# Conditioning in column groups, scans of two segments with ScalarE carries, unpadded heads in layer 3

## Time and profile before

| | |
|---|---|
| three runs | 8062.61, 8064.74 (median), 8066.53 us |
| profiled execution | 8064.97 us; its span, first to last instruction, 8063.2 us |
| busy in the span | PE 7071.7 us (88%), PEld 3761.9, DVE 6189.8 (77%), ACT 5870.7 (73%), POOL 2286.7 (28%) |
| mean granted clock of TensorE | 0.954 of 2.4 GHz |

### The profile page before, as it was taken

The page is one execution under the profiler, slowest core; times in us unless marked ns, Lnnn a source line. Parts: engine busy times, 40 slices in busy tenths (PEclk is TensorE's granted clock), DMA queues, the critical chain, the costliest instruction groups (busy, mean ns, idle before and its releaser), DMA issues. The chain is left out here.

```text
span 8063.2 us, 233691 instructions
## 1 busy us (share of the span) xinstructions
PE 7071.7 (88%) x94272; PEld 3761.9 (47%) x94272; DVE 6189.8 (77%) x4829; ACT 5870.7 (73%) x7834; POOL 2286.7 (28%) x1375
## 2 busy tenths in 40 slices
PE   7999588888888888888888888887989999979998
PEld 5444244444444444444444444444435454535554
DVE  2555499999999999999999999998434353445554
ACT  2555499999999999999999999996224343435544
POOL 0000133333333333333333333332003232323332
PEclk9999699999999999999999999998999999989999
DMA  4666522222222222222222222222520000000000
GB/s 151 151 155 146 117 70 67 64 68 67 70 66 66 67 68 69 66 66 68 67 67 66 68 68 67 67 64 98 200 81 9 6 9 8 6 32 9 12 11 6
DMA packets 621116, 541.43 MB, mean 67 GB/s; under 512 B 490224, under 2 KB 528752, under 8 KB 606448
## 3 DMA queue, kind: packets, MB, share of 16 engines
q1 hardware_dynamic: 620032, 526.35, 22.5%
HBM read 380.72 MB, written 145.49 MB: 65 GB/s over the span
## 5 line engine op out<-in xcount | busy, mean ns | idle before, releaser
L1267 DVE TENSOR_TENSOR_SCAN s_h<-s_decay,s_h 128x1040 f32<-128x1040 f32 x2048 | 4623.9, 2336 | 33.8 <-ACT s_decay L1191 33.8
L1162 ACT COPY s_h<-s_pb 128x1024 f32<-128x1024 f32 x2048 | 2506.0, 1224 | 111.1 <-PE s_pb L1093 92.2
L1106 PE MATMUL s_py<-s_h,s_cz 128*32 128x128 f32 x32768 | 2512.9, 436 | 6.1 <-DVE s_h L1267 6.1
L1191 ACT ACTIVATE s_decay<-s_pa 128x1024 f32<-128x1024 f32 x2048 | 2139.4, 1045 | 123.6 <-DVE s_h L1267 53.4
L1234 POOL TENSOR_TENSOR s_h<-s_h,s_one 128x64 f32<-128x64 f32 x384 | 875.3, 2279 | 2079.3 <-DVE s_h L1267 2079.3
L1078 PE MATMUL s_pa<-s_dl,s_al 18*128 18x64 bf16 x32768 | 857.8, 192 | 673.7 <-ACT s_decay L1191 584.9
L1106 PEld LDWEIGHTS s_py<-s_h,s_cz 128*32 128x32 f32 x32768 | 1036.5, 123 | 469.3 <-issue 10.0
L1078 PEld LDWEIGHTS s_pa<-s_dl,s_al 18*128 18x128 bf16 x32768 | 612.8, 95 | 1019.9 <-ACT s_decay L1191 953.4
L1093 PEld LDWEIGHTS s_pb<-s_ul,s_bl 18*128 18x128 bf16 x16384 | 475.3, 95 | 1031.3 <-ACT s_h L1162 877.5
L1093 PE MATMUL s_pb<-s_ul,s_bl 18*128 18x128 bf16 x16384 | 838.1, 222 | 27.7 <-ACT s_h L1162 16.0
L1222 POOL TENSOR_TENSOR s_cz<-s_cl,s_one 128x128 f32<-128x128 f32 x256 | 434.3, 1697 | 964.2 <-PE s_py L1106 952.4
(11 more groups left out here) (223 smaller groups left out, 6219.2 us busy)
## 6 DMA issues: line engine op xcount, KB each, us to landing
s_bl<-B SPq DMA_DIRECT2D x1024, 72.0 KB
s_ul<-U SPq DMA_DIRECT2D x1024, 72.0 KB
s_dl<-D SPq DMA_DIRECT2D x1024, 72.0 KB
s_al<-A SPq DMA_DIRECT2D x256, 144.0 KB
D<-p_dp SPq DMA_DIRECT2D x64, 384.0 KB, 6.5
U<-p_up SPq DMA_DIRECT2D x64, 384.0 KB, 5.6
B<-p_bz SPq DMA_DIRECT2D x144, 128.0 KB, 2.2
SZ<-p_sz SPq DMA_DIRECT2D x16, 1024.0 KB, 5.1
```

The source lines that it names most:

```text
L1106: mm = pe.matmul(py[e % 2][QR * q:QR * q + QR, 0:P], cz[e % 2][:, l * P + QR * q:l * P + QR * q + QR], states, start=(l == 0), stop=(l == ...
L1162: act.copy(out, pb[:].rearrange("p b t d -> p d b t")).then_inc(bu_done, 1)
L1191: act.activation(decay[(STEPS * e + 2 * z + j) % RING][:, :, 1:W], pa[j % 2][:], ACT.Exp).then_inc(exp_done, 1)
L1267: dve.tensor_tensor_scan(seg, decay[(STEPS * e + 2 * z + j) % RING][:].rearrange("p d w -> p (d w)"), seg, 0.0, ALU.mult, ALU.add).then_in ...
```

## The change

**conditioning.** `cond`, `hid` and `sil` are padded to 32 columns and become the weights everywhere: the 4096 outputs of `w2a` and `w2b` are cut into four groups of 1024, `mod` into three of 1536, and each group writes its own 32 partitions of PSUM. `w2a` and `mod` are then turned back by transposes. SP loads `w2a` and `w2b` ahead of `wm`, PE does `mod` last. `az` outlives the stage, and its 18 stores stand in `prepare` behind `reload(0)`. POOL sets the zeros and the identity.

**scan.** A scan covers STRIDE = 2 steps, 2080 elements, HALVES = 4 scans a tile; `decay` has RING = 3 buffers of 32 channels x 65, the same memory. The carry is ACT's, in two copies of 64 channels after the exps of steps 0 and 4, for the tiles that have one before them in their sequence. POOL zeroes column 0 of the first tile of a sequence in one operation, and keeps the fill.

**transformer.** Layer 3 has HR = 16: HT = 8 heads a tile, MT = 2, PT = 4. The padded arrays still come from the host: SP loads the padded `Wqkv3` into `hid`, and DVE, ACT and POOL copy one of q, k and v each into `wqkv` without the padding; `wo` and a small `bias` come in 8 DMAs each. The zeros around a head in `vt` are shared. In both layers the slices of projections move by one job: `MIDDLE = 5`.

```diff
@@ conditioning
-                for m in range(32):
-                    for k in range(FC):
-                        mm = pe.matmul(pw[:, 0, m * NB:(m + 1) * NB], w2a[:, k, m * P:(m + 1) * P],
-                                       hid[:, k, :], start=(k == 0), stop=(k == FC - 1))
-                mm.then_inc(wa_mm, 1)
...
+                def group(out, g, j, weights, k, moving, at):
+                    return pe.matmul(out[GB * g:GB * (g + 1), j, :], weights[:, k, :],
+                                     moving[:, k, 512 * at:512 * (at + 1)], start=(k == 0), stop=(k == FC - 1))
...
+                for j in range(2):
+                    for k in range(FC):
+                        for g in range(4):
+                            mm = group(pw, g, j, hid, k, w2a, 2 * g + j)
+                    mm.then_inc(wa_mm, 1)
...
+                pe.wait_ge(wm_in, 64)
+                for j in range(3):
+                    for k in range(FC):
+                        for g in range(3):
+                            mm = group(pm, g, j, sil if g else cond, k, wm, 3 * g + j)
+                    mm.then_inc(mod_mm, 1)
+                for j in range(3):
+                    pe.wait_ge(modr_done, j + 1)
+                    for q in range(4):
+                        mm = pe.transpose(pm[:, j, q * P:q * P + 3 * GB], modr[0:3 * GB, j, q * P:(q + 1) * P],
+                                          ident[0:3 * GB, 0:3 * GB])
+                    mm.then_inc(modt_mm, 1)
@@ prepare, SyncE
                 reload(0)
+                for j in range(PARTS):
+                    for m in range(PARTS):
+                        for b in range(PAIR):
+                            sp.dma_start(scratch["A3"][:, m, j, b].rearrange("n d f -> d n f"),
+                                         keep["az"][:, :, m, b].rearrange("p n c s -> p n (c s)")).then_inc(s["a_out"], 16)
@@ scan
-    RING = 6
+    STRIDE = 2
+    HALVES = STEPS // STRIDE
+    RING = 3
...
-        decay = [sb(f"decay{e}", [P, FG, W]) for e in range(RING)]
+        decay = [sb(f"decay{e}", [P, STRIDE * FG, W]) for e in range(RING)]
@@ scan, ScalarE
+                def carry(k, to, before, g):
+                    rows = slice(P // 2 * g, P // 2 * (g + 1))
+                    wait(act, scanned, HALVES * (k - 1) + HALVES // 2 * (g + 1))
+                    act.copy(hb[to][:, rows, 0], hb[before][:, rows, TB]).then_inc(carried, 1)
...
-                            wait(act, scanned, STEPS * k + j + 1 - RING)
-                            act.activation(decay[(STEPS * e + 2 * z + j) % RING][:, :, 1:W], pa[j % 2][:], ACT.Exp
+                            at = j // STRIDE
+                            wait(act, scanned, HALVES * k + at + 1 - RING)
+                            part = slice(FG * (j % STRIDE), FG * (j % STRIDE + 1))
+                            act.activation(decay[(z + e + at) % RING][:, part, 1:W], pa[j % 2][:], ACT.Exp
                                            ).then_inc(exp_done, 1)
+                            if e and j in (0, STEPS // 2):
+                                carry(k, (z + e) % HB, (z + e - 1) % HB, 2 * j // STEPS)
                             if not (last and e == NT - 1):
                                 take_bu(*ahead(n, e, 1), (z + e + 1) % HB, j)
@@ scan, GpSimd
-                def carry(n, e, z):
...
+                def clear(n, z):
+                    wait(pool, scanned, HALVES * (NT * n - HB + 1))
+                    pool.tensor_tensor(hb[z][:, :, 0], zcol[:], one[:].to_broadcast([P, P]), ALU.mult
+                                       ).then_inc(cleared, 1)
@@ scan, VectorE
-                        for j in range(STEPS):
...
+                        for j in range(HALVES):
+                            if e == 0 and j == 0:
+                                wait(dve, cleared, n + 1)
+                            if e and j % (HALVES // 2) == 0:
+                                wait(dve, carried, 2 * ((NT - 1) * n + e - 1) + j // (HALVES // 2) + 1)
+                            wait(dve, exp_done, STEPS * k + STRIDE * (j + 1))
+                            rows = slice(STRIDE * FG * j, STRIDE * FG * (j + 1))
+                            seg = hb[to][:, rows, :].rearrange("p d w -> p (d w)")
+                            dve.tensor_tensor_scan(seg, decay[(z + e + j) % RING][:].rearrange("p d w -> p (d w)"),
                                                    seg, 0.0, ALU.mult, ALU.add).then_inc(scanned, 1)
@@ transformer
-    HR, dh = (DH2, DH2) if layer == 2 else (PADH, DH3)
+    HR, dh = (DH2, DH2) if layer == 2 else (DH3, DH3)
...
+    MIDDLE = 5
...
                     if more:
-                        project(i + 1, slice(3, 4))
+                        project(i + 1, slice(3, MIDDLE))
                     wait(pe, s["x2h"], i + 1)
                     linear(i, "mean2", [(ones[:], x2h[:])])
                     if more:
-                        project(i + 1, slice(4, 6))
+                        project(i + 1, slice(MIDDLE, MIDDLE + 2))
                     wait(pe, s["q2h"], i + 1)
                     linear(i, "var2", [(ones[:], q2h[:])])
                     if more:
-                        project(i + 1, slice(6, qkv.count))
+                        project(i + 1, slice(MIDDLE + 2, qkv.count))
...
+                if layer == 3:
+                    dve.wait_ge(s["wqkv_in"], 16)
+                    dve.tensor_copy(*columns_of(0)).then_inc(s["wq"], 1)
```

More of the change, by code:

```diff
@@ L1712, in _ @@
                 load(0, 0)
-                weights(wqkv, f"Wqkv{layer}")
-                weights(wo, f"Wo{layer}")
+                if layer == 2:
+                    weights(wqkv, "Wqkv2")
+                    weights(wo, "Wo2")
+                else:
+                    unpadded()
                 weights(w1, f"W1{layer}")
@@ L1857, in _ @@
                 pe.wait_ge(s["wqkv_in"], 16)
+                if layer == 3:
+                    for n in "qkv":
+                        pe.wait_ge(s["w" + n], 1)
                 pe.wait_ge(s["h1"], 4)
```

271 lines of the change are left out of this document (149 added, 122 removed).

## The result

The changed kernel takes **7934.69 us** (median of 4 runs, 7928.42 to 7936.31) against 8064.10 us before (4 runs, 8062.61 to 8066.53): ratio 0.9838, 95% interval 0.9821 to 0.9855. The profiled execution took 7928.42 us with a span of 7926.6 us, 136.6 less than the span of before; the medians differ by 129.4. The kernel was profiled again beside the layer-3 experiments (after_again: median 7931.87 us, profiled span 7933.4), and from the two profiles one sees how far stages move by themselves: the conditioning ended at 54.3 and 56.5 us, the second stage took 873.3 and 877.8, the scan 4546.0 and 4543.4. So differences of 2 to 5 us of a whole kernel say nothing; those within a stage are read from the traces. Of the four runs the profiled one was the fastest, so the sums over its trace come out some 6 us better than the median.

The account below looks back on a forecast made before the run. DVE's scans were taken to bound the scan, 4626 of 8063 us, with PE bounding conditioning. Scan -85, conditioning -44, layer 2 -11 and layer 3 0 sum to -140: 8065 - 140 = 7925 us, range 7875 to 7995.

Parts of the forecast that it names:

- scan, start to start of undisturbed scans: Scan, DVE: 1024 scans at 4.38 us instead of 2048 at 2.217, a gain of 55 us (bounds 4 and 168).
- scan, POOL relief: Scan: carries gone from POOL and fewer clears disturb DVE less, a gain of 46 us (bounds 20 and 55).
- scan, first pair and disturbances: Scan: 16 us against the gain (bounds 0 and 70), from the first pair, small disturbances and loop turns.
- conditioning: Conditioning: loads become the bound instead of PE, next stage starts at 58 instead of 102, -44 us (-34 to -48).
- layer 2: Layer 2: one more projection fills PE's wait ahead of mean2, -1.5 us in seven units, -11 (-4 to -12).
- layer 3, start: Start of layer 3: four projections fewer, -7 us, and +1 for waits on the unpacking copies.
- layer 3, units and end: Layer 3: 1.6 us a unit gained, slow clock costs 0.8 x 3.8, +10 in seven units; last unit keeps 3.5.
- The fixed part of a scan: Scan, DVE: 0.06 us of each scan doesn't depend on its length, so 2080 elements cost about 4.38 us.
- The forecast 17.6 against 17.7: Scan: time per tile in us, ACT 17.6 with the carries against DVE 17.7, so DVE still ends last.
- the lead of 5.5 us: Scan: ACT ends an exp 5.5 us before DVE needs it with three paired buffers, 10.2 with the ring of 6.
- the term for small disturbances: Scan: 11 us lost to small disturbances between ACT and DVE, two nearly equal engines, 0.04 us a tile.
- The price of the clock: Layer 3: PE's gaps bring the 1.2 GHz clock; mean2 and var2 1 us longer each, f0 onwards 2, in most units.

Follow-up runs that it names:

- l2_middle: The changed kernel with MIDDLE = 4 in layer 2, as before, and 5 in layer 3: 7938.4 us, ratio 0.9842 to the kernel before.
- acarry_only: The kernel before with only the carries moved to ScalarE, in two copies; scans of 1040 elements and ring of 6 kept: 8029.2 us, ratio 0.9954.
- The spare matmuls: The changed kernel with unused matmuls in two PE gaps of layer-3 units, ahead of the waits for x2h and h2: 7919.9 us, ratio 0.9822.
- the new order: The changed kernel with DVE in layer 3 taking only q0 ahead of the residuals: 7905.7 us; with unused matmuls in PE's gaps too, 7892.7 us.

## Why the prediction was right

Forecast 7925, measured 7934.69. By its steps, each against the profiled spans:

| step | forecast | measured |
|---|---|---|
| scan, start to start of undisturbed scans | -55 | -52 (2047 x 2.216 to 1023 x 4.383) |
| scan, POOL relief | -46 | -33 (85.4 to 52.0) |
| scan, first pair and disturbances | +16 | +8 (idle 5.7, last scan 2.2 longer) |
| conditioning | -44 | -47.6 |
| layer 2 | -11 | -11.5 (l2_middle) |
| layer 3, start | -6 | -7.7 (19.2 less 11.5) |
| layer 3, units and end | +6.5 | +9.3 |
| prepare and finish_scan | 0 | -1 |

By the spans the gain is 136.6 us where 140 were forecast, by the medians 129.4. That the sum came so near is in part luck: POOL's relief fell 13 us short and the scans 3, and the disturbances and the conditioning came out 8 and 4 us better.

*The fixed part of a scan.* It was 0.05 us (2 x 2.216 - 4.382), forecast 0.06 from two operations of another kind. The interpolation held.

*POOL.* The mechanism was right, the size off in one term, the clears. Fills and clears were put at 0.12 each, their mean in the kernel before, so that half the clears would save 8 us. By the starts of the scans a fill costs 0.164 us, before and after. A clear of 64 elements cost 0.054 (6.8 us for all of them), and a clear of 128 costs 0.164, as much as a fill (10.3 us for all). So one large clear in place of two small ones cost 3.5 us more, and 33 us came instead of 46. acarry_only confirms the carries' part to 1 us. The clears of before, as a group, and then two scans and a clear of the changed kernel:

```profile
L1238 POOL TENSOR_TENSOR s_h<-s_zcol,s_one 128x64 f32<-128x64 f32 x128 | 290.6, 2301 | 0.1
```
```profile
3049.31 4.62 DVE L1314 TENSOR_TENSOR_SCAN s_h<-s_decay,s_h 128x2080 f32<-128x2080 f32 x1
3053.85 4.62 DVE L1314 TENSOR_TENSOR_SCAN s_h<-s_decay,s_h 128x2080 f32<-128x2080 f32 x1
3049.54 4.63 POOL L1281 TENSOR_TENSOR s_h<-s_zcol,s_one 128x128 f32<-128x128 f32 x1
```

The clear ends 0.3 us into the scan of 3053.85, which lasts 4.62 us instead of the 4.46 of a scan at whose start no POOL operation ends; at the start of the scan of 3049.31 a fill ends, with the same effect.

*ACT.* The forecast 17.6 against 17.7 and the lead of 5.5 us (measured: median 5.4, before 10.05) describe the stage. The 16 us against the gain were 2 for the first pair, 11 for small disturbances and 3 for the turns of the loop. Measured are 4.3 us at the turns, 1.4 of waits for the clear behind them, 2.2 for the longer last scan, and nothing between: the term for small disturbances was too large.

*Conditioning.* Loads bound it, as forecast. The last load let PE go at 42.5 where 39.6 was forecast, and the 18 matmuls on wm took 6.8 us where I had taken 10 (bounds 6 and 18): the groups overlap nearly in full, even though the granted clock was 0.51 for the first 3.5 us of them (records of 1.06 us, later 0.59). From them to the next stage it is 5 us instead of 8. So a miss of 3 us one way and two of 3 us the other way stand behind the -47.6.

*Layer 3.* That 7 x 10.7 us of PE's work would bring nothing was the main statement, and it held: the time from the first take to mean2 was forecast as 11.5 and is 11.3 to 11.45, to var2 as 16.3, and it is 16.2 to 17.4. The step that failed is a smaller one, the last of the chain: f0 was to come 22.8 us after the first take, 1.6 earlier than before, and comes 22.7 only in the seventh unit, in the others 23.6 to 25.4. The mean is 24.0 against 24.5 before, a gain of 0.6. Two things were missing. The table load of 1.3 us stands behind the wait for var2 in one of the two units of the loop's body; I had followed a unit of before in which it stood ahead. And the slow clock already slows the projections between mean2 and var2, so that var2 comes up to 0.95 us later (17.42 instead of 16.47). On average these are 0.4 and 0.5 us a unit, about the 1.0 that is missing. In the unit shown the gaps, forecast as 4.0, 2.1 and 4.7, are 3.96, 0.79 and 5.97.

The price of the clock was forecast well in sum. The 16 matmuls from f0 on take 8.7 to 10.2 us instead of 7.1, 2.4 us more on average where 2 were forecast; var2 comes 0.5 later on average and mean2 not at all, where 1 each was forecast. That is 2.9 us a unit against 0.8 x 3.8 = 3.0. The seven periods grew by 12 us instead of 10, and the last unit gave back 2.9 instead of 3.5. The spare matmuls won 13 us of layer 3 in six units, alone as well as on top of the new order, so 2.2 us a unit could be had back. The Trainium skill (TensorE: Matmul & The Clock Gate, HAM oscillation — how this bites in real kernels) has the slow clock come back each time round: it did, in all seven units.

*Not tried.* Whether the ring of three pairs could be made longer, to hide the loop turns again, wasn't tried; it would be worth at most 5.7 us. Nor was a clear in two halves on the merged scans, worth 3.5 us by the prices above, an estimate. The unpadded heads of layer 3 were never run without the rest of the change, so what they do is read from the traces.

## What to carry to other kernels

Work taken off the busiest engine is worth only what the chain beside it lets go: before halving matmuls, follow the engine that empties their banks, and put its reads in the order in which the chain needs them, not in that in which they are made. Where a gap on TensorE can't be closed, see what the granted clock does behind it, and try matmuls for nothing in it; chain and clock are two losses and are mended separately. When an operation moves from one engine to a nearly bounding other, measure the margin by doing it twice or three times there.
